# One-core decoder block with routed experts: another order of work between the attention loop and the first expert tiles

## What is computed

```python
x = x + rbf_attention(_layernorm(x))             # softmax over exp(-|q-k|^2), then @ Wo + bo
x = x + cross_attention(ctx, ctx, _layernorm(x)) # 16 heads of 16, mask, softmax, @ Wo + bo
x = x + moe(_layernorm(x))                       # 8 experts, top 2, 256 -> 1024 -> 256
...
gate_logits = xs @ Wg
weights, sel = jax.lax.top_k(gate_logits, 2)
weights = softmax(weights)
h = relu(einsum('td,edf->etf', xs, W1) + b1)     # only the two picked experts count
out = weights[0] * out_e[sel0] + weights[1] * out_e[sel1]
```

## Time and profile before

| | us |
|---|---|
| median of 3 runs | 601.18 |
| lowest, highest | 601.0, 604.86 |
| span of the profiled execution | 601.1 |
| TensorE busy in it | 543.9 (90%) |
| VectorE, ScalarE, GpSimd busy | 389.9, 331.4, 241.8 |

### The profile page before, as it was taken

The page is one execution under the profiler, slowest core; times in us unless marked ns, Lnnn a source line. Parts: engine busy times, 40 slices in busy tenths (PEclk is TensorE's granted clock), DMA queues, the critical chain, the costliest instruction groups (busy, mean ns, idle before and its releaser), DMA issues.

```text
span 601.1 us, 15268 instructions
## 1 busy us (share of the span) xinstructions
PE 543.9 (90%) x5443; PEld 470.4 (78%) x5443; DVE 389.9 (65%) x880; ACT 331.4 (55%) x663; POOL 241.8 (40%) x300
## 2 busy tenths in 40 slices
PE   4878899999999999878976999999999999999991
PEld 3876668777877777554555999999999999999991
DVE  5788867879696967667567787862332455655551
ACT  4653367665556575514733945556555667575660
POOL 6452213223231321000526544445445636777443
PEclk9999899999999999976986999999999999999996
DMA  7687550816355352740557856667778555545532
GB/s 230 189 101 139 91 70 5 135 28 115 48 92 70 64 97 34 112 142 22 159 178 239 269 167 167 185 177 185 199 175 241 118 138 120 144 107 122 133 64 26
DMA packets 56184, 76.63 MB, mean 127 GB/s; under 512 B 6704, under 2 KB 44880, under 8 KB 56112
## 3 DMA queue, kind: packets, MB, share of 16 engines
q1 hardware_dynamic: 46848, 64.55, 43.2%
q0 software_dynamic: 7872, 10.33, 10.6%
q10 hardware_dynamic: 1392, 0.79, 0.4%
HBM read 53.00 MB, written 9.31 MB: 104 GB/s over the span
## 4 chain that ended last, share of the span: by engine, by line
PE 65%; DVE 9%; DMA 8%; ACT 7%; issue 5%; POOL 3%; SPq 1%; DVEq 0%; POOLq 0%; ACTq 0%
PE bank L1419 15%; PE pair L2946 11%; PE bank L3002 8%; PE pair L1419 5%; DMA w_now<-L_ffn_W 5%; PE bank L1847 5%; PE pair L1697 4%; PE pair L1810 4%; PE bank L2832 2%; DVE row_max L1750 2%; PE pair L1738 2%; PE bank L1361 1%; ACT hid L2800 1%; PE bank L1942 1%; DMA x<-x 1%
## 5 line engine op out<-in xcount | busy, mean ns | idle before, releaser
L1750 DVE TENSOR_REDUCE row_max<-pair 128x4 f32<-128x1024 f32 x64 | 77.7, 1221 | 17.9 <-PE pair L1738 17.8
L2946 PE MATMUL pair<-slots_t,w_now 128*128 128x128 f32 x672 | 80.8, 280 | 0.6 <-DMA w_now<-L_ffn_W 0.6
L2946 PEld LDWEIGHTS pair<-slots_t,w_now 128*128 128x128 f32 x672 | 79.0, 197 | 0.8 <-DMA w_now<-L_ffn_W 0.8
L1827 ACT ACTIVATE exp_ring<-pair 128x1024 f32<-128x1024 f32 x64 | 64.9, 1027 | 25.5 <-PE pair L1810 22.6
L2976 ACT ACTIVATE hid<-pair,b_tile 128x128 f32<-128x128 f32 x168 | 47.5, 366 | 31.7 <-PE pair L2946 28.7
L2899 POOL DMA_INDIRECT out<-y,scatter_now x21 | 34.4, 1638 | 70.7 <-DVE y L3016 52.1
L2954 DVE TENSOR_TENSOR hid_lo<-hid,hid_hi 128x1024 fp32r<-128x1024 f32 x21 | 25.8, 1229 | 49.0 <-ACT hid_hi L2983 42.5
L2706 POOL DMA_INDIRECT out<-y,scatter_now x18 | 31.9, 1770 | 38.4 <-DVE y L3016 18.4
L3002 PE MATMUL bank<-experts_w,hid_hi 128*128 x336 | 44.4, 284 | 0.0
L1295 POOL TENSOR_SCALAR rstd<-moments 128x2 f32<-128x2 f32 x24 | 7.6, 316 | 89.8 <-DVE moments L1292 89.8
L3002 PEld LDWEIGHTS bank<-experts_w,hid_hi 128*128 128x128 f32 x336 | 40.8, 188 | 0.0
(11 more groups left out here) (349 smaller groups left out, 1460.4 us busy)
## 6 DMA issues: line engine op xcount, KB each, us to landing
w_now<-L_ffn_W SPq DMA_DIRECT2D x21, 1024.0 KB
w_now<-L_ffn_W SPq DMA_DIRECT2D x18, 512.0 KB
experts_w<-L_ffn_W SPq DMA_DIRECT2D x8, 1024.0 KB, 6.9
k_stack<-ck_hi SPq DMA_DIRECT2D x32, 128.0 KB, 4.3
q_stack<-cq_hi SPq DMA_DIRECT2D x32, 128.0 KB, 4.2
ctx_in<-ctx SPq DMA_DIRECT2D x8, 256.0 KB, 2.8
k_stack<-ck_lo SPq DMA_DIRECT2D x16, 128.0 KB, 5.4
q_stack<-cq_lo SPq DMA_DIRECT2D x16, 128.0 KB, 4.8
```

What stands on the lines that cost most here:

```text
L1750: core.e["maxed"].at(eng.tensor_reduce(maxima, pair[:, :].rearrange("p (c t k) -> p c t k", c=KT, t=KT), AX.X, ALU.max))
L1827: core.e["exp"].at(eng.activation(slots.rearrange("p c t q -> p (c t q)"), pair[:, :], ACT.Exp, scale=HD ** -0.5))
L2946: mm = eng.matmul(banks[half][:, f * P:(f + 1) * P], core.w1_now[b.p][:, c, start:start + P], core.slots_t[b.p][:, c, :], start=c == 0, st ...
```

## The change

The three last stages of loop step 7 leave the loop. The drain of each engine has a new order: the maxima of batch 6 and the two other stages stand among the score tiles, which are issued one by one; the 16 exponential tiles of batches 6 and 7 follow in one series, one by one, with group 0's routing beside them. The routers of batches 5, 6 and 7 and all weight splits but that of expert 1 stand among the first expert tiles, as does the transpose and output of batch 7; each of the first eight tiles waits only for the splits that it needs (`WATCHED`). Group 1's routing is one step later. The router has bank 7, `y` and the normalised rows of batch 7 have other places, with the waits that this needs.

```diff
@@ plan_late_experts: y moves to the place of batch 7's residual rows
+WATCHED = 8
...
@@ attention_tensor, _scalar, _vector, ahead of their last stages
+    if it.v == LAST_BATCH.v:
+        return
...
@@ def drain_tensor(core, eng): (all of the new order; b6 = at(1), b7 = at(0))
+    last_maximum(at, 0)
+    at(1, st_maxima)
+    last_maximum(at, 1)
+    at(2, st_weighted, 3)
+    at(0, st_cross_value)
+    last_maximum(at, 2)
     at(2, st_heads_transposed)
+    last_maximum(at, 3)
+    last_maximum(at, 4)
+    last_maximum(at, 5)
+    last_maximum(at, 6)
+    prefix_product(core, eng, 0)
     at(2, st_transpose, "hT")
+    last_maximum(at, 7)
+    last_exponential(at, 1, 0)
+    last_exponential(at, 1, 1)
+    at(0, st_maxima)
+    at(1, st_weighted, 0)
+    last_exponential(at, 1, 2)
+    last_exponential(at, 1, 3)
     at(2, st_output)
+    last_exponential(at, 1, 4)
     at(1, st_weighted, 1)
+    last_exponential(at, 1, 5)
+    last_exponential(at, 1, 6)
     at(1, st_weighted, 2)
-    at(2, st_router_transpose)
+    last_exponential(at, 1, 7)
+    last_exponential(at, 0, 0)
     at(1, st_weighted, 3)
-    at(2, st_router)
+    last_exponential(at, 0, 1)
+    table_product(core, eng, 0, 0)
+    last_exponential(at, 0, 2)
+    at(0, st_weighted, 0)
+    last_exponential(at, 0, 3)
+    table_product(core, eng, 0, 1)
     at(1, st_heads_transposed)
+    last_exponential(at, 0, 4)
+    at(0, st_weighted, 1)
+    last_exponential(at, 0, 5)
+    table_product(core, eng, 0, 2)
     at(1, st_transpose, "hT")
+    last_exponential(at, 0, 6)
     at(0, st_weighted, 2)
     table_product(core, eng, 0, 3)
     b1_transpose(core, eng)
+    last_exponential(at, 0, 7)
+    at(1, st_output)
+    at(0, st_weighted, 3)
+    at(0, st_heads_transposed)
-    at(0, st_transpose, "hT")
@@ def drain_scalar(core, eng): (its end)
     at(0, st_exps, 6)
     at(0, st_exps, 7)
+    split_expert(core, "scalar", eng, 1)
     at(0, st_weighted, 3)
@@ def drain_vector(core, eng): (all of the new order from the second tile on)
+    at(1, st_maxima)
+    at(0, st_scores, 1)
+    at(0, st_cross_value)
+    at(0, st_scores, 2)
+    at(3, st_best)
+    at(0, st_scores, 3)
     routing_choice(core, "vector", eng, 0)
     at(2, st_heads_transposed)
+    at(0, st_scores, 4)
+    at(0, st_scores, 5)
+    at(0, st_scores, 6)
     at(2, st_transpose, "hT")
+    at(0, st_scores, 7)
     at(0, st_maxima)
     routing_counts(core, "vector", eng, 0)
     routing_rows(core, "vector", eng, 0)
     routing_weights(core, "vector", eng, 0)
     routing_hot(core, "vector", eng, 0, 0)
+    routing_hot(core, "vector", eng, 0, 1)
+    first_tiles(core, "vector", eng)
+    at(2, st_output)
+    routing_hot(core, "vector", eng, 0, 2)
+    routing_hot(core, "vector", eng, 0, 3)
+    routing_values(core, "vector", eng, 0, 3)
+    at(1, st_heads_transposed)
+    at(2, st_moments, 2)
     at(2, st_normalise, 2)
+    routing_index(core, "vector", eng, 0)
     at(1, st_transpose, "hT")
     at(1, st_output)
     at(0, st_heads_transposed)
@@ def drain_gpsimd(core, eng):
+    routing_values(core, "gpsimd", eng, 0, 0)
+    routing_values(core, "gpsimd", eng, 0, 1)
+    routing_values(core, "gpsimd", eng, 0, 2)
     at(2, st_moments, 2)
@@ def drain_sync(core, eng):
     load_expert(core, eng, 2)
+    experts_sync(core, eng)
     at(0, st_maxima)
     at(2, st_output)
...
     core.e["p_hT"].wait(eng, LAST_BATCH)
-    load_expert(core, eng, 4)
...
-        load_expert(core, eng, x)
@@ def experts(core, name, eng, it): (sync: loads 4, 5, 6 at n = 2, 3, 4)
@@ tensor
         if n == 1:
-            st_output(core, name, eng, LAST_BATCH, it)
+            st_transpose(core, name, eng, LAST_BATCH, it, "hT")
         at(1, ex_rows_t)
         at(2, ex_hidden)
         if n == 2:
+            st_output(core, name, eng, LAST_BATCH, it)
+            st_router_transpose(core, name, eng, LAST_BATCH.back(2), it)
+        elif n == 3:
+            st_router(core, name, eng, LAST_BATCH.back(2), it)
+            st_router_transpose(core, name, eng, LAST_BATCH.back(1), it)
+        elif n == 4:
             st_router_transpose(core, name, eng, LAST_BATCH, it)
+        at(3, ex_out)
         if n == 3:
+            st_router(core, name, eng, LAST_BATCH.back(1), it)
+        elif n == 4:
             st_router(core, name, eng, LAST_BATCH, it)
+        elif n == 5:
             prefix_product(core, eng, 1)
...
@@ vector
         at(1, ex_bias)
         if n == 0:
+            st_moments(core, name, eng, LAST_BATCH.back(1), it, 2)
+            st_transpose(core, name, eng, LAST_BATCH, it, "hT")
+            split_expert(core, name, eng, 1)
+            st_normalise(core, name, eng, LAST_BATCH.back(1), it, 2)
             st_output(core, name, eng, LAST_BATCH, it)
             st_moments(core, name, eng, LAST_BATCH, it, 2)
+        elif n == 1:
+            st_router(core, name, eng, LAST_BATCH.back(2), it)
+            split_expert(core, name, eng, 2)
             st_normalise(core, name, eng, LAST_BATCH, it, 2)
+        elif n == 2:
+            st_best(core, name, eng, LAST_BATCH.back(2), it)
...
@@ def st_normalise, batch 7 (its rows go to batch 6's place)
+        elif b.v == NB - 1:
+            core.e["ln2"].wait(eng, b.back(1))
+            eng.wait_ge(core.E["residual_before"], 16)
@@ def ex_hidden_first
+    if isinstance(b.v, int) and b.v == 0:
+        core.e["p_y2"].wait(eng, LAST_BATCH)
@@ def ex_out, tensor
-        if isinstance(b.v, int) and b.v < 3:
+        if isinstance(b.v, int) and b.v < WATCHED:
             eng.wait_ge(core.split["lo"], core.splits)
-        elif isinstance(b.v, int) and b.v == 3:
+        elif isinstance(b.v, int) and b.v == WATCHED:
             eng.wait_ge(core.split["lo"], NE)
-        if isinstance(b.v, int) and b.v == 1:
-            core.e["gate"].wait(eng, LAST_BATCH)
+        if isinstance(b.v, int) and b.v == 0:
+            core.e["x2"].wait(eng, LAST_BATCH)
@@ def ex_out, vector, first tile
-            core.xn_stored.wait(eng, LAST_BATCH)
+            eng.wait_ge(core.E["residual_out"], 16)
+            core.e["ln2"].wait(eng, LAST_BATCH)
```

237 lines of the change are left out of this document (103 added, 134 removed).

## The result

The changed kernel takes 593.63 us, median of 4 runs (590.55 to 598.33), beside 602.22 for the kernel before in the same group of runs: ratio 0.9887, with a 95% interval of 0.984 to 0.9933. In a second group of runs it took 596.15 (0.9893, 0.9854 to 0.9932). The forecast was 590.5 and "faster by over 1%"; both measurements lie at 1.1%, just beyond that bound, with intervals that reach across it: that it is faster is clear, that it is faster by over 1% is not. (The time of a run is its profiled span plus 2.1 us: 596.2 belongs to the run of 598.33, the slowest of the four, and 601.1 of before to one of 603.26. The forecast put the span of before at the median; its 590.4 is a span and would be a time of 592.5.)

A forecast was written before the change was run, and what follows sets the result against it. The drain was taken to lose 19.5 us to TensorE pauses and up to 18.6 to half speed. From 601.1, minus 20.2 (8.5 + 15.3 - 3.6), plus 2 for handoffs and 7.5 for clock: 590.4, stated 590.5; range 582 to 599.

The forecast's parts named there:

- signs of being right: Time ranges for drain points from last maximum to third output, with the first gather right behind the index; then 244 us.
- signs of being wrong: Series clock under 0.7, TensorE pauses over 3 us in tiles 0-3, row wait at tile 13, or gain lost by the end.
- (a): Last maxima in the drain: work placed between score tiles fills VectorE's time; last maximum at 268.6, 6.9 us sooner.
- (b): Exponential series in the drain: starts before the last maximum, at 267.1; last weighted product at 297.5, 8.5 us sooner.
- (c): Passage from last weighted product to first expert product: routing lies under the exponentials; 5.4 us instead of 20.7, 15.3 won.
- (d): First expert product to third output: added batch 7 output and routers, waits for splits and bias; 33.5 us, 3.6 lost.
- bound by VectorE: First expert tiles: VectorE's work serialises with the routers, or the index is late; 6 us lost, 596.5; chance 0.18.
- three stretches of 5 us: Low TensorE clock expected behind pauses in the drain's new order: 7.5 us lost, ends 0 and 18.6.
- as low as before: Drain: 37 us of low TensorE clock remain and give back 18.6 us; 601.5, no change; chance 0.09.
- The bias loads: Sixteen loads issued earlier on SP, before the last maxima's stores: no cost, unless late by more than 4 us.
- The slower case: TensorE stays at 1.2 GHz from 253 through the series into the first tiles; 52 us of it give 609; chance 0.05.
- The loads did not bound the expert part: Feared outcome: third output 15 us sooner but the kernel's end not, meaning loads bound the expert part.

The follow-up runs named there:

- the clock aided: Changed kernel plus matmuls whose result nobody reads, issued in TensorE's pauses among the drain's score tiles and before a weighted product: 589.5 us, ratio 0.978.
- the kernel with the choice moved: Changed kernel with VectorE's routing choice and heads of batch 5 behind the sixth score tile's maximum instead of the fourth's: 593.78 us, ratio 0.9893.
- orders alone: Changed kernel with three reorderings (routing choice later, table products earlier, first tiles' router transposes and bias copy earlier), no added matmul: 584.69 us, ratio 0.9736.
- unread matmuls: Changed kernel with matmuls nobody reads in TensorE's pauses, plus the first-tiles reordering and earlier table products: 584.36 us, ratio 0.9721.

## Why the prediction was right, and where it was not

By direction and range it held: faster, 593.63 in 582 to 599, 3.1 us above the value. By ratio it forecast 590.4 / 601.1 = 0.982 and got 0.989, so some 4 us of the 10.7 forecast are missing. The steps held less well than the number. Of the points named as signs of being right, five lie later than their ranges in both profiles: last maximum 273.5 and 274.1 (269 to 272), last weighted product 309.7 and 308.0 (298 to 304), index 307.3 and 305.6 (296 to 302), first expert product 9.8 and 11.4 us sooner (15 to 24), third output 4.4 and 6.0 us sooner (11 to 20). Only the distance from there to the end came as forecast. That the time still fell into the range is due to the width of the range as much as to the account. None of the signs of being wrong came either. The steps:

- **(a) Last maxima: the waits were mis-sized.** 6.9 us sooner was forecast, 2.0 measured, with the loop's end 1.24 later. From that end it is 18.7 us against 15.1: VectorE's work is 14.0 (forecast 13.6), its waits 4.7 (forecast 1.5). The largest, 2.08 us, is for the cross value, which TensorE issues behind a weighted product that took 1.93 us at 1.2 GHz; with the clock aided this wait is 0.71, all waits 2.0 and the stage 15.8. The pause ahead of the seventh tile was sized well (2.6 us by my estimate, 2.41 measured). That (a) makes the kernel faster is not shown: with it undone the time is the same.
- **(b) Series: the step that failed, by its clock.** 30.4 us from its first tile at 267.1 were forecast. It starts at 272.13 and takes 37.6: at a granted clock of 0.81 it spends 2 x 0.19 x 37.6 = 14.3 us at the low level and loses 7.1 there; 34.5 busy - 7.1 = 27.4 us of work (forecast 26.4) and 3.1 of pauses (forecast 4.0; the first, 1.46, was put at 1.4). So work and waits were sized well, and the excess of 7.2 us is the clock: the place where I had counted on "26 us of work in 30, and the row of the same density has 0.93". The series started at 1.2 GHz and left it at 286.1, 14 us in. With the clock aided it starts 0.8 us later than forecast and takes 34.9, of which 1.7 is low clock and 1.9 the added transposes.
- **(c) Passage: right in kind, 1.8 us short.** It takes 7.2 us against 5.4 (20.7 before). The index is not behind the series any more; but from index to landed rows it is 315.51 - 307.34 = 8.2 us where the rows of before had 5.45: GpSimd issued the first gather at 308.40 and the rows took 7.1 us (4.4 before). SP had issued weight loads at 306.91 and 308.10 and the DMA share is 0.86 to 1.11 from 308 to 316; that they delay the rows is not shown. Gathers and heads do arrive together, as forecast, within 2.25 us. These 13.5 us are the one large gain, of which the series and the first tiles give part back; no run undid this step alone, so that it carries the gain is read from the profiles.
- **(d) First tiles: close by the sum, for another reason.** 35.3 us against 33.5 and 29.9 before. The forecast's own terms add up to 30.7 and not 30, so 34.2 with the 3.5 us for splits. In place of splits it was the wait of the bias copy and the half speed behind it: with the router's transposes and products and one bias copy moved and all splits in place, the part takes 30.8 us. This is the rival "bound by VectorE", but by one wait in its queue, not by its work: VectorE is busy 31.8 of 49.5 us.
- **The clock.** 7.5 us were charged as three stretches of 5 us, with ends 0 and 18.6. The stretch at the seventh tile alone was 20 us long. Counted in the windows, half speed costs 16.9 us, hardly less than the 18.9 of before, so as a count the rival "as low as before" was right. As a price it was not: aiding the clock gives 6.6 us. The count treats every half-speed microsecond as one on the path: for a regained clock I had credited 11 us of the 18.6 of the kernel before, and there an aid that took the count down by 12 gave 4. Some of it is on the path: in both kernels the stage of the last maxima is 3 to 4 us shorter at full clock. What the rest of the counted time did is not shown.

The bias loads, taken at nothing, cost nothing here: SP issued the last of them by 268.4 and the stores of the last maxima at 275.83. One gather took 2.82 us beside a split (1.14 alone), as the row of before had it.

The Trainium skill (TensorE: Matmul & The Clock Gate, What's actually happening) says the throttled state is the default and activity lifts it. The trace agrees in that the 20 us at 0.50 ended while TensorE was busy without a pause, 2.00 of each 2 us from 278 to 286. It was just as busy from 268 to 272, and there the clock did not come back. In the kernel with the choice moved the full clock was lost behind pauses of 0.29 to 0.55 us.

The slower case did not come: low clock in the series is there, but TensorE left it at 286 and regained it twice in the first tiles, at 320 and at 337. The loads did not bound the expert part, and the distance from the third output to the end is the same, as forecast (244). What remains open is whether a drain at full clock over the score tiles and also without the gather's wait would beat 584.4; no run had both.

The best versions beat both kernels: 584.69 us with orders alone and 584.36 with unread matmuls, 0.974 and 0.972 of before.

## What to carry to other kernels

Where two engines take turns, as the maxima and the score tiles do here, moving work among the tiles changed nothing that the runs can tell (undoing (a), moving the choice); what paid was to find the one copy or transpose in the queues of the next stage on which the others stand (here a bias copy and a router's transposes, 4.4 us, and table products, 4.3 us). Price a low clock by what filling the pauses gives in a run, not by half of its duration: a count of 11.4 us less gave 6.6 here, one of 12 us less gave 4. A gain ahead of a wait for a DMA can shrink at that wait, and more if the clock falls in it (5.2 us at the end of the series, 2.7 at the end of the span, in one pair of profiles). Before two profiles are compared at a point, look whether they enter the stage at the same time: here they differ by up to 3 us.
